# A deformable convolution with attention and experts: products of zeros where TensorE would wait

## The reference

```python
off1 = conv2d(x, w_off1, b_off1, stride=1, pad=1)
out = relu(bn_inf(deform_conv(x, off1, w_dc1, 1, 2, 2), g1, beta1, m1, v1))
off2 = conv2d(out, w_off2, b_off2, stride=1, pad=1)
out = bn_inf(deform_conv(out, off2, w_dc2, 1, 2, 2), g2, beta2, m2, v2)
x = relu(out + x)
t = _to_tokens(x)                                  # (8, 1024, 64)
t = t + _L1_attn_ref(_ln_t(t), Wq, Wk, Wv, Wu, bu)     # 8 heads, window of 32 tokens
t = t + _L1_ffn_ref(_ln_t(t), gate_w, gate_b, weight1, weight2)
```

## Time and profile before

| | us |
|---|---|
| median of 3 runs | 719.65 |
| lowest and highest | 715.48, 722.56 |
| the profiled execution, its own time | 723.8 |
| its span, first to last instruction | 722.0 |
| PE busy, share of the span | 617.2, 85% |
| DVE busy | 439.8, 61% |
| ACT busy | 359.7, 50% |
| mean granted TensorE clock, share of full speed | 0.861 |

### The profile page before, as it was taken

One profiled execution on the slowest core, in us unless ns is written; L12 is line 12 of the kernel. 1 busy time (PEld: TensorE's weight loads), 2 busy tenths in 40 slices (PEclk: granted clock), 3 DMA queues, 4 the chain that ended last, 5 costly groups with the idle time before them and its releaser, 6 DMA issues.

```text
span 722.0 us, 31347 instructions
## 1 busy us (share of the span) xinstructions
PE 617.2 (85%) x14342; PEld 456.7 (63%) x14342; DVE 439.8 (61%) x662; ACT 359.7 (50%) x570; POOL 135.0 (19%) x183
## 2 busy tenths in 40 slices
PE   7469999989694998898987598999999999994576
PEld 2136667666521776677766476888888888873353
DVE  0568789889326866566544435666676666756524
ACT  0254667666315555455442434565665656653541
POOL 4000111111100000000000604434434344331400
PEclk9855999999986598888897557999999999998758
DMA  8320000000004000000003600000000000000002
GB/s 298 82 51 3 5 5 5 5 4 5 6 15 88 4 5 4 5 5 4 5 4 81 189 1 1 3 0 0 0 0 0 0 0 0 0 1 1 1 1 118
DMA packets 6979, 18.11 MB, mean 25 GB/s; under 512 B 1933, under 2 KB 4301, under 8 KB 6149
## 3 DMA queue, kind: packets, MB, share of 16 engines
q1 hardware_dynamic: 6862, 16.37, 8.3%
HBM read 12.50 MB, written 3.87 MB: 23 GB/s over the span
## 4 chain that ended last, share of the span: by engine, by line
PE 75%; DVE 8%; ACT 5%; issue 5%; DMA 4%; SPq 2%; POOL 1%; DVEq 0%; POOLq 0%; ACTq 0%
PE banks L285 19%; PE banks L216 11%; PE banks L883 9%; PE banks L860 5%; PE banks L927 5%; PE banks L908 5%; PE banks L942 4%; PE banks L188 3%; PE banks L202 2%; DMA off<-in_places_dram 2%; PE banks L873 2%; PE banks L636 1%; DMA off<-offsets_dram 1%; DVE y L320 1%; ACT y L320 1%
## 5 line engine op out<-in xcount | busy, mean ns | idle before, releaser
L285 PE MATMUL banks<-y,xt 32*64 32x144 f32 (+4 forms) x6656 | 148.7, 287 | 16.9 <-issue 6.5
L285 PEld LDWEIGHTS banks<-y,xt 32*64 32x64 f32 x6656 | 105.9, 146 | 49.3 <-issue 26.5
L341 DVE TENSOR_TENSOR y<-hy,hx 128x576 f32<-128x576 f32 (+4 forms) x208 | 108.7, 585 | 4.6
L368 ACT ACTIVATE hx<-banks 128x576 f32<-128x576 f32 (+1 forms) x96 | 58.4, 610 | 65.0 <-PE banks L188 63.2
L216 PE MATMUL banks<-y,w_dc 64*64 64x128 f32 x2304 | 85.7, 302 | 5.8 <-issue 4.1
L216 PEld LDWEIGHTS banks<-y,w_dc 64*64 64x64 f32 x2304 | 75.9, 152 | 12.5 <-issue 10.6
L320 DVE COPY y<-banks 128x768 f32<-128x768 f32 x48 | 45.8, 955 | 60.9 <-PE banks L285 60.9
L1046 DVE TENSOR_REDUCE stats<-banks 128x16 f32<-128x1024 f32 x32 | 39.2, 1224 | 69.5 <-PE banks L883 69.5
L1124 POOL TENSOR_TENSOR y<-y,stats 128x1024 f32<-128x1024 f32 x32 | 60.8, 1900 | 109.2 <-DVE stats L1056 109.2
L373 ACT ACTIVATE hy<-banks 128x768 f32<-128x768 f32 (+3 forms) x92 | 64.9, 732 | 22.2 <-PE banks L202 21.4
L883 PEld LDWEIGHTS banks<-src,y 64*128 64x128 f32 x1024 | 64.5, 201 | 7.9 <-issue 7.9
(11 more groups left out here) (144 smaller groups left out, 798.6 us busy)
## 6 DMA issues: line engine op xcount, KB each, us to landing
y<-in_w_dram SPq DMA_DIRECT2D x1, 2080.0 KB
xt<-in_xt_dram SPq DMA_DIRECT2D x1, 2048.0 KB, 10.2
off<-in_w_dram SPq DMA_DIRECT2D x2, 1024.0 KB
out_dram<-tokens SPq DMA_DIRECT2D x4, 512.0 KB, 2.6
offsets_dram<-tokens SPq DMA_DIRECT2D x32, 54.0 KB
off<-offsets_dram SPq DMA_DIRECT2D x16, 108.0 KB
src<-in_x_dram SPq DMA_DIRECT2D x4, 306.0 KB, 3.9
src<-in_x_dram SPq DMA_DIRECT2D x4, 272.0 KB, 5.5
```

The source lines that it names most:

```text
L285: last = nc.tensor.matmul(ap(out, [[UNIT_ROWS * PITCH - 2, 3], [PITCH, strip.n], [1, cols]]), m.xt[32 * j:32 * j + 32, strip.tile_row, c, ...
L341: multiply(dst, hy, hx, ALU.mult).then_inc(cv.s_ready[g], 1)
L368: nc.scalar.activation(ap(m.hx[:, u % 2, 0, n * item[2]:], [[X_HATS, 2], [2 * n, 3], [1, n]]), ap(m.ps[:, bank, :], [[BANK, 2], [n, 3], [1 ...
```

## The change

Nothing that is computed for the output changes. TensorE gets extra products of `m.zeros` with itself (`keep_busy`, 128x512, one instruction each), whose results no engine reads (they leave zeros in the banks):

- while the path is chosen: 12 ahead of the maximum's product, and 30 (first convolution) or 8 (second) behind it, before the wait for the offsets;
- among the first distances: 2 behind each of the items 1 to 6, into banks 0 to 3. Two DVE memsets that put zeros at the edges of these banks, with their semaphore, in the second convolution, go;
- between units: a "w" item of 5 products (3 where a "t" item stands) behind each unit that has no final product, that is the units of row 0 and each unit (row, 2). With it, all distances of unit u + 2 move `inside`, the y items too;
- in the first normalisation: 4 behind the turning back of pair 1, and 8 behind those of pairs 2 and 3, after a wait until all four pairs are centred.

The wait for `off_ready` moves ahead of the first distances. For the second convolution the wait for `m.turned` stands ahead of the zeros as well.

```diff
--- before.py
+++ after.py
@@ -40,6 +40,9 @@
 IMAGES = [[0, 2, 4, 6], [1, 3, 5, 7]]
 ROW_COORD, ROW_ONE, ROWS_OFF = 12, 13, 14
 FIRST_BANK = 4
+RING_BANKS = range(FIRST_BANK, FIRST_BANK + 4)
+
+BUSY_MOVES = [30, 8]
 
 UNIT_ROWS = TILE_ROWS
 PLACES = UNIT_ROWS * W
@@ -126,6 +129,7 @@
 
 
 
+
     def __init__(self, turns, window):
         self.units, strips, self.window = [], 0, window
         for u in range(len(UNITS)):
@@ -138,17 +142,17 @@
             todo = self.units[unit.u + 2].coords if unit.u + 2 < len(UNITS) else []
             final = [("f", row - 1, ky)] if row and ky < 2 else []
             turn = [("t", row - 2)] if turns and row >= 2 and ky == 2 else []
-            cut = len(todo) if final else (len(todo) + 1) // 2
-            unit.inside, unit.behind = todo[:cut], final + turn + todo[cut:]
+            wait = [] if final else [("w", unit.u, 3 if turn else 5)]
+            unit.inside, unit.behind = todo, final + turn + wait
             if unit.u == len(UNITS) - 1:
-                unit.behind = unit.behind + [("f", row, 0), ("f", row, 1)]
+                unit.behind = turn + [("f", row, 0), ("f", row, 1)]
                 if turns:
                     unit.behind = unit.behind + [("t", row - 1), ("t", row)]
             self.items = self.items + unit.inside + unit.behind
 
         self.count, kinds = {}, {}
         for item in self.items:
-            kind = item[0] if item[0] in "ft" else "xy"
+            kind = item[0] if item[0] in "ftw" else "xy"
             kinds[kind] = kinds.get(kind, 0) + 1
             self.count[item] = kinds[kind]
 
@@ -159,6 +163,14 @@
 
 class Conv:
     pass
+
+
+def keep_busy(nc, m, banks, n):
+
+    for k in range(n):
+        last = nc.tensor.matmul(m.ps[:, banks[k % len(banks)], :], m.zeros[:, 0:P], m.zeros[:, :], start=True, stop=True,
+                                skip_group_check=True)
+    return last
 
 
 def ring_banks(n):
@@ -253,7 +265,8 @@
         if n >= 2:
             last = cv.plan.items[n - 2]
             done = {"f": cv.finished, "t": m.turned}.get(last[0], cv.emptied)
-            pe.wait_ge(done, cv.plan.count[last])
+            if last[0] != "w":
+                pe.wait_ge(done, cv.plan.count[last])
         bank = ring_banks(n)
         if item[0] == "x":
             if item[1:] == (3 * HALF_ROWS // UNIT_ROWS, 0):
@@ -267,6 +280,8 @@
             if cv.k and item[1:] == (0, 0):
                 pe.wait_ge(m.w_scaled, 1)
             final_pe(nc, m, cv, bank, item[1], item[2])
+        elif item[0] == "w":
+            keep_busy(nc, m, (bank, bank + 1), item[2]).then_inc(cv.filled, 1)
         else:
             pe.wait_ge(m.staged, PAIRS * (item[1] + 1))
             turn_pe(nc, m, bank, item[1]).then_inc(cv.filled, 1)
@@ -290,14 +305,15 @@
         if c == TC - 1:
             last.then_inc(cv.sampled, 1)
 
+
+    pe.wait_ge(cv.off_ready, 8)
     for n in range(cv.plan.first):
         item_pe(n)
+        if n:
+            keep_busy(nc, m, (2 * n % PAIRS, (2 * n + 1) % PAIRS), 2)
     n = cv.plan.first
-    pe.wait_ge(cv.off_ready, 8)
     if cv.k:
         pe.wait_ge(m.turned, TR)
-    if cv.plan.window.inset:
-        pe.wait_ge(m.edges, 2)
     for unit in cv.plan.units:
         groups = [(strip, c) for strip in unit.strips for c in range(TC)]
         if unit.u:
@@ -348,6 +364,8 @@
 def sampler_act(nc, act, m, cv):
     def item_act(n):
         item = cv.plan.items[n]
+        if item[0] == "w":
+            return
         bank = ring_banks(n)
         act.wait_ge(cv.filled, n + 1)
         if item[0] == "f":
@@ -418,11 +436,6 @@
                 weigh(nc.vector.tensor_tensor, dve, m, cv, unit, strip, g)
 
     units = cv.plan.units
-    if cv.plan.window.inset:
-
-        dve.wait_ge(cv.off_ready, 8)
-        for at in (4, 2 * UNIT_ROWS * PITCH + W + 3):
-            nc.vector.memset(ap(m.ps[:, 0, at:], [[BANK, PAIRS], [PITCH, UNIT_ROWS]]), 0.0).then_inc(m.edges, 1)
     hats(units[0])
     weights(units[0])
     hats(units[1])
@@ -733,7 +746,7 @@
     pass
 
 
-def norm_pe(nc, pe, m, ln, beside):
+def norm_pe(nc, pe, m, ln, beside, busy=False):
 
     for pr in range(PAIRS):
         if ("turn", pr) in beside:
@@ -756,6 +769,10 @@
             last = nc.tensor.transpose(m.ps[:, 4 * (pr % 2) + 2 + b // 4, b % 4 * P:(b % 4 + 1) * P],
                                        ln.xt[pr][:, b, :], m.identity[:, :])
         last.then_inc(ln.back_in_psum, 1)
+        if busy and pr:
+
+            pe.wait_ge(ln.centred, PAIRS)
+            keep_busy(nc, m, (0, 1), 4 if pr == 1 else 8)
 
 
 def norm_act(nc, act, m, ln, beside):
@@ -1428,7 +1445,6 @@
             convs.append(cv)
 
         m.w_scaled = sem("w_scaled")
-        m.edges = sem("edges")
         m.xt_loaded = sem("xt_loaded")
         m.staged, m.turned = sem("staged"), sem("turned")
         source_rows = places[1][:, 0:PAIRS * HP * WP].rearrange("p (i r c) -> p i r c", i=PAIRS, c=WP)
@@ -1737,8 +1753,12 @@
                 if cv.k == 0:
                     pe.wait_ge(loaded, NLOAD)
                     pe.wait_ge(m.xt_loaded, 16)
+                if cv.k:
+                    pe.wait_ge(m.turned, TR)
+                keep_busy(nc, m, RING_BANKS, 12)
                 pe.wait_ge(cv.max_ready, 5)
                 nc.tensor.transpose(m.ps[0:1, 0, 0:P], m.abs_max[:, 4:5], m.identity[:, :]).then_inc(cv.max_turned, 1)
+                keep_busy(nc, m, RING_BANKS, BUSY_MOVES[cv.k])
                 pe.wait_ge(cv.moved[0], MOVES)
                 pe.wait_ge(cv.flag_ready, 1)
                 flag = nc.tensor.value_load(far_flag[0:1, cv.k:cv.k + 1], min_val=0, max_val=1)
@@ -1764,7 +1784,7 @@
                 last.then_inc(heads_in_psum, 1)
 
             pe.wait_ge(convs[1].finished, FINALS - 1)
-            norm_pe(nc, pe, m, at.ln, {("turn", 2): head_products, ("back", 0): lambda: pe.wait_ge(heads_ready, 2)})
+            norm_pe(nc, pe, m, at.ln, {("turn", 2): head_products, ("back", 0): lambda: pe.wait_ge(heads_ready, 2)}, True)
             pe.wait_ge(at.ln.normed, PAIRS)
             attention_pe(nc, pe, m, at)
             experts_pe(nc, pe, m, ex)
```

## The result

The changed kernel takes 731.44 us (median of 3 runs, 731.35 to 735.51) against 719.65. The ratio is 1.021, with an interval of 1.011 to 1.031: slower, where 692 us was forecast, though whether it is slower by 2% is open. A fourth execution, of 738.61 us, is in the ratio and not in the median; the medians alone give 1.016. The profiled execution took 735.5 us, 11.7 more than the one of before.

A forecast was written before the change was run, and what follows sets the result against it. TensorE, partly at half clock, was taken to bound the second convolution, and DVE nearly the first. Terms 0 - 0.3 + 4.4 + 2.5 - 2.3 + 3.9 + 12.0 + 7.2 = 27.4 us off 719.65 gave 692, range 683 to 706.

The forecast's parts named there:

- The first choice of path: First convolution's start: 12 and 30 zeros fit into TensorE's idle time; cost 0, bounds 0 to 5.6 us.
- worth 4 us at the first final product: First convolution, row 0: full clock and y items inside save 2.8 us, the first final product 1.6; 4.4 together.
- The first distances of the second convolution: Zeros among them overrun TensorE's idle time if the clock falls; cost 2.3 us, bounds 0.3 to 3.4.
- the 3.9 for row 0: Second convolution, row 0: 2.3 us from fewer DVE waits plus 1.6 from a faster first final product.
- Rows of the first convolution: Rows 1 to 7: y items inside remove about half of DVE's 5.6 us of waits; gain 2.5 us.
- Rows of the second convolution: Turn zeros hold the clock, saving 14.1 us, less 2.1 for order; net gain 12.0, bounds 3 to 14.
- the weak place: Second convolution, unit (row, 1), narrowest products and no zeros: clock may fall in a row or two, 3 us each.
- The normalisation: First normalisation: zeros raise the clock, so queries and scores run faster; gain 7.2 us, bounds 3 and 9.
- zeros don't act on the clock: Rival: zeros are only added work everywhere; 20 us slower, 740 us; chance 0.05.
- transposes don't count: Rival, normalisation: transposes don't count as busy, attention starts later and first groups stay at half; 696 us; chance 0.06.
- The clock is held in part: Rival: clock falls in half the second convolution's rows, its row 0 stays half, normalisation gives 4; 704 us; chance 0.20.
- DVE and ACT take over: Rival, both convolutions: DVE's waits only move, row 0 gives only final products, first convolution's rows nothing; 700 us; chance 0.14.

The follow-up runs named there:

- b_start_placed: Kernel before plus zeros at both path choices and among first distances, cuts put back with 74 and 94 one-column products: 722.79 us, 1.000.
- b_start_norm: Kernel before plus zeros at path choices, first distances and first normalisation, none at turns, cuts put back: 720.47 us, 0.995.
- a_zeros_first: Changed kernel, cuts put back, y items behind the unit again and the turn's zeros ahead of them: 726.08 us, 1.004 of the kernel before.
- a_placed: Changed kernel with 74 and 60 one-column products that put the cuts back at each convolution's start: 726.75 us, 1.012 of the kernel before.
- a_no_turn_zeros: Changed kernel without zeros between units, y items inside, cuts put back: 732.87 us, 1.014 of the kernel before.
- b_pad64: Kernel before plus 64 one-column products in TensorE's wait for its first loads: 754.87 us, 1.048.
- b_pad127: Kernel before plus 127 one-column products, a whole block, ahead of the offsets: 722.14 us, 1.003.
- b_start: Kernel before plus only the zeros at both path choices and among the first distances, cuts not put back: 739.45 us, 1.021.
- b_order: Kernel before with only the y items moved inside, no zeros anywhere: 738.95 us, 1.023.
- a_hold: `a_placed` plus 4 more products of zeros inside each unit (row, 1) of the second convolution: 731.50 us, 1.012 of the kernel before.
- a_zeros_first_2: `b_start_norm` plus the turn's zeros in the second convolution only, cuts put back: 728.29 us, 1.002 of the kernel before.
- b_norm: Kernel before plus only the 20 zeros of the first normalisation: 715.92 us, 0.994.

## Why the prediction was wrong, point by point

**The sum.** With the cuts put back, adjacent versions differ by one part each (a difference of two ratios, each taken within its own set of runs; 1% is 7.2 us):

| version | ratio | what it adds | us |
|---|---|---|---|
| `b_start_placed` | 1.000 | choices of path, first distances | 0 |
| `b_start_norm` | 0.995 | the normalisation's zeros | -3.5 |
| `a_zeros_first` | 1.004 | the turn's zeros | +6.3 |
| `a_placed` | 1.012 | the y items inside | +5.8 |
| the change | 1.021 | the cuts where the change leaves them | +6.3 |

The steps are of the size of their intervals (0.3 to 1%), and single-part runs agree in sign for each. Their size depends on what else is there: the y items inside cost 1.9% without the turn's zeros (`b_start_norm` to `a_no_turn_zeros`) and 0.8% with them, and with the y items inside the turn's zeros cost nothing (1.014 to 1.012). The cuts are put back for the start of each convolution; where a row has more products they still creep.

- **The step that failed first is one the prediction doesn't have.** It priced each product by its duration and its place and wrote "Cost 0" for those in a wait. An instruction also moves every later cut of the instruction stream. `b_pad64` (+4.8%) and `b_pad127` (+0.3%) show that alone, and `b_start` (1.021, with the cuts put back 1.000) for a part of the change. The rows of "issue" were in the trace of before, 6.5 us before the sampling, and I didn't ask what made them. The cuts are some 0.9% of the 2.1%; the two steps named below, on the rows, are the rest.
- **The first choice of path.** The mechanism held: the clock is whole from 11.9 us to 206.5 us, and the first distances start at 38.7 instead of 39.06 us. Cost 0 in its place, as said. That it was worth 4 us at the first final product also shows (63.3 against 67.4). In `b_start_norm` the trace has it too (63.7), and loses it again between the convolutions: from the last final product of the first to the first one of the second it takes 60.9 us, where before takes 56.9. That is the start of the second convolution, next.
- **The first distances of the second convolution.** The clock did fall in the wait for the DMA. I took 2.3 with bounds to 3.4; it is 8.0 - 4.4 = 3.6, since the pairs took 1.03 us and nothing overlapped. Of the 3.9 for row 0, the 1.6 of the first final product came (2.2 us against 4.0) and the 2.3 didn't: from the first sampling to it are 18.6 us, where before has 18.8, with the clock at half from 230 to 247 us.
- **Rows of the first convolution: "Inside, they are there before it" (+2.5).** DVE's waits for y distances did go (over the whole span 11.7 us before, 2.4 after). The step left out the other side of ACT's order: its `take` comes later by the same items, and TensorE waits for that, 19.7 us in `b_order`. By the starts of final products `b_order` loses 5 us before the first one, 3 in these rows, 3 between the convolutions, 4 in the rows of the second and 2 behind them. So the term was about -3 and not +2.5 (bounds -2 and 5), and the greater loss lies in row 0 and the second convolution, where the prediction priced this order at a gain and at 2.1 us.
- **Rows of the second convolution: 12.0 us, measured none.** The step was "If that holds the clock". It doesn't: the weak place was named, unit (row, 1), but priced at "a row or two"; the clock fell seven times between 264 and 395 us, and from 262 to 382 us it is 0.87, where before it was 0.86. The zeros only moved the place of half speed. The rate, 42%, was near enough (37% for the sampling products, 47% for the final ones). The price of the zeros was not: I set 5 products against 0.74 us of wait and called the rest free, and left out the stops. With the cuts put back, where the clock does rise (0.89 in `a_placed`, 0.93 in `a_hold`), the zeros' own time and longer stops take back what it gives. `a_zeros_first_2`, these zeros alone, gains nothing over `b_start_norm`.
- **The normalisation: 7.2, measured 4.3** (`b_norm`, 721.1 x 0.006; bounds 3 and 9). The mechanism is right and only its size was off: as foreseen the clock falls again behind the scores (at 445 us), and where TensorE is faster its waits for ACT and DVE between queries and scores grow (0.9, 1.2 and 1.7 us, where before had 0.6 and 0.9).
- **The rivals.** That zeros don't act on the clock is refuted by each trace. That transposes don't count: for the first normalisation this can't be judged, since the zeros stood between the transposes in every run that had them; the kernel before still speaks against it, with the clock at 0.50 from 672 to 675 us, transposes alone on TensorE, and at 1.00 from 676 us. The Trainium skill, TensorE: Matmul & The Clock Gate, Part 4 (PE-mode transpose), has them not counting as busy in the same way. "The clock is held in part" came true for the second convolution. "DVE and ACT take over" was near in kind: DVE's waits did move, from y distances to TensorE's sampling (17.7 us against 5.7), but by ACT's place for its `take` and the stops, not by DVE's busy share. The prediction had no rival in which useful work stays the same and the stream of instructions shifts.

## What to carry to other kernels

Before costing added instructions at nothing, look for "issue" stops at a fixed distance in the engine's timeline: if there are any, an edit must be compared with the cuts put back (pad with as many tiny instructions as complete the period), or else its own effect can't be told from the shift. Before pricing a fill with zeros at the rate of the clock, look whether the clock holds to the end of the stretch, and set against it the zeros' own time and the stops that a faster engine still meets; fill with zeros only a wait that stays a wait, and not the path from a copy to the next unit. When an item is moved ahead on one engine, follow it on the engine that empties it: what that engine does later is someone's wait.

## What the runs showed of the hardware that I had not expected

- TensorE's stops for "issue" in the convolutions lie multiples of 126 or 127 products apart (with their weight loads twice as many instructions), at some of the cuts only: 8 of some 40 in the first convolution before, 24 after. They last 0.3 to 1.5 us each, 6.2 to 14.3 us before the sampling products depending on where the cuts fall, and each of the 401 longer ones ends 1.2 to 1.6 us after a 16 KB transfer of the instruction queue (98 in the page) has ended. 64 one-column products changed the time by 4.8%, 127 by 0.3%. That the block of instructions is what TensorE waits for is inferred from the period and the transfers' times.
- Products of zeros hold the clock and raise it: 1.00 without a break from 11.9 to 206.5 us. Each takes 0.21 us at full (30 in 6.64 us, the last one's tail in it) and 0.43 to 0.5 us at half (two in 1.03 us).
- The narrow sampling products follow the clock nearly as the wide ones do: 32 of 90 columns take 0.90 us at half and 0.57 us at full, while 72 final products take 4.12 and 2.20 us.
